# First stage of a six-stage decoder kernel: query weights in four column groups, and the loads and vector work in another order

## What is computed

```python
x = _layernorm(x + _L0_attn_ref(x, Wq, Wk, Wv, Wo))
x = _layernorm(x + _L0_xattn_ref(x, ctx, ...))
x = _layernorm(x + _L0_ffn_ref(x, ...))
x = _layernorm(x + _L1_attn_ref(x, ...))
x = _layernorm(x + _L1_xattn_ref(x, ctx, ctx, ...))
x = _layernorm(x + _L1_ffn_ref(x, ...))
```

```python
q = (x @ Wq).reshape(b, n, H, HD).transpose(0, 2, 1, 3)
k = (x @ Wk).reshape(b, m, HKV, HD).transpose(0, 2, 1, 3)
v = (x @ Wv).reshape(b, m, HKV, HD).transpose(0, 2, 1, 3)
q = q * cq + rotate_half(q) * cq
k = k * ck + rotate_half(k) * ck
attn = jax.nn.softmax(jnp.einsum('bhnd,bhmd->bhnm', q, k) * scale)
out = jnp.einsum('bhnm,bhmd->bhnd', attn, v)
return out.transpose(0, 2, 1, 3).reshape(b, n, H * HD) @ Wo
```

## Time and profile before

| | |
|---|---|
| time, median of 3 runs | 2896.91 us (2895.69 to 2898.89) |
| profiled execution, its own time | 2890.31 us |
| its span | 2888.5 us |
| PE busy | 2667.9 us, 92% |
| DVE, ACT, POOL busy | 1879.2, 1311.8, 1248.2 us |
| mean granted clock of PE | 0.965 |
| moved by DMA | 49.16 MB |

### The profile page before, as it was taken

How to read it: one execution, slowest core, us unless ns; L and a number is a source line. 1 busy time by engine, 2 the same in 40 slices (tenths; PEclk the granted TensorE clock), 3 DMA queues, 4 the chain that set the end, 5 groups by cost and what they waited for, 6 DMA issues and landing times. The chain is left out here.

```text
span 2888.5 us, 65059 instructions
## 1 busy us (share of the span) xinstructions
PE 2667.9 (92%) x23764; PEld 2306.1 (80%) x23764; DVE 1879.2 (65%) x4014; ACT 1311.8 (45%) x3138; POOL 1248.2 (43%) x1605
## 2 busy tenths in 40 slices
PE   6999999994999999999999889996999999699995
PEld 5999999994888888888888768885777777477774
DVE  5555556554777777777777654444777777366766
ACT  2222222223666666666666533332433334266665
POOL 3111121122576777777676501113455454334444
PEclk9999999997999999999999989997999999799998
DMA  4000000002000000000000020001000000000001
GB/s 144 8 7 7 4 7 7 7 0 99 6 4 5 4 4 5 4 5 4 5 4 5 0 75 0 0 0 33 9 8 11 7 11 0 26 27 26 29 12 59
DMA packets 42507, 49.16 MB, mean 17 GB/s; under 512 B 4032, under 2 KB 33600, under 8 KB 41920
## 3 DMA queue, kind: packets, MB, share of 16 engines
q1 hardware_dynamic: 42432, 48.16, 5.0%
HBM read 35.56 MB, written 4.19 MB: 14 GB/s over the span
## 5 line engine op out<-in xcount | busy, mean ns | idle before, releaser
L528 POOL TENSOR_TENSOR a_probs<-a_probs,a_rs 128x512 f32<-128x512 f32 x64 | 66.8, 1044 | 482.4 <-DVE a_rs L421 482.4
L1109 POOL TENSOR_TENSOR b_rows<-b_rows,b_swapped 128x512 f32<-128x512 f32 x160 | 204.4, 1286 | 56.0 <-DVE b_swapped L895 55.9
L1050 ACT ACTIVATE b_probs<-bank,b_shift,b_q_scale 128x128 f32<-128x128 f32 x512 | 228.2, 461 | 0.7
L1156 POOL TENSOR_TENSOR b_probs<-b_probs,b_rs 128x512 f32<-128x512 f32 x128 | 133.2, 1040 | 137.0 <-DVE b_rs L947 133.8
L2593 ACT ACTIVATE d_probs<-d_probs 128x512 f32<-128x512 f32 x128 | 78.9, 630 | 242.7 <-DVE d_probs L2492 240.8
L485 ACT COPY a_pT<-bank 128x512 f32<-128x512 f32 x64 | 37.5, 586 | 326.3 <-PE bank L300 326.3
L46 PE MATMUL bank<-a_xT,a_wq 128*128 128x256 f32 x512 | 150.3, 293 | 26.4 <-DVE a_xT L388 26.4
L1119 POOL TENSOR_TENSOR b_rms<-b_rms,sh_minus_half 128x8 f32<-128x8 f32 (+1 forms) x128 | 169.6, 1325 | 10.7
L903 DVE TENSOR_REDUCE b_ss<-b_squares 128x4 f32<-128x512 f32 x192 | 125.2, 680 | 73.7 <-ACT b_squares L1025 73.7
L46 PE MATMUL bank<-b_wo,b_oT 128*128 128x256 f32 x512 | 150.8, 295 | 1.4 <-DVE b_oT L869 1.4
L426 DVE TENSOR_TENSOR a_oT<-bank,a_oT 128x512 fp32r<-128x512 f32 x128 | 82.5, 686 | 103.2 <-ACT a_oT L490 103.2
(11 more groups left out here) (350 smaller groups left out, 8923.8 us busy)
## 6 DMA issues: line engine op xcount, KB each, us to landing
a_xT_in<-in_xT SPq DMA_DIRECT2D x16, 256.0 KB, 2.7
sh_x<-in_x SPq DMA_DIRECT2D x1, 4096.0 KB, 24.9
b_ctx_in<-in_ctxT SPq DMA_DIRECT2D x32, 128.0 KB, 2.0
d_x_in<-sh_x SPq DMA_DIRECT2D x16, 256.0 KB, 2.3
e_x_in<-sh_x SPq DMA_DIRECT2D x16, 256.0 KB, 2.3
e_cT<-in_ctxT SPq DMA_DIRECT2D x32, 128.0 KB, 2.5
out<-sh_x SPq DMA_DIRECT2D x16, 256.0 KB, 2.1
a_qT<-in_L_attn_Wq SPq DMA_DIRECT2D x1, 2048.0 KB, 8.5
```

The costliest lines, as they stand in the source:

```text
L1050: op = act.activation(probs[:, g % 2, keys], bS[:, keys], ACT.Exp, bias=shift[:, g % 2, a:a + 1], scale=q_scale[:, g, a // 2, a % 2:a % 2 ...
L1109: pool.tensor_tensor(rows[:, unit, :], rows[:, unit, :], swapped[:, half, :], ALU.add).then_inc(added[unit], 1)
L1156: pool.tensor_tensor(pr, pr, rs[:, g % 2, :].unsqueeze(2).to_broadcast([128, R, 128]), ALU.mult).then_inc(probs_ready[g], 1)
```

## The change

The loads. Wq is loaded in four groups of 512 columns, in the order group 0, x turned, group 1, the tables, groups 2 and 3, Wk, Wv, Wo. Then SP waits for the first low part of x, issues x turned of turn 1 and, behind it, x in rows. The 24 semaphore increments are made by ACT and POOL, 12 each.

The weights. Each group of Wq is folded (two DVE instructions over both chunks of rows), rounded and split by itself, and so is Wk; Wk's fold also takes two instructions instead of four. Wo is rounded on ACT, after Wv, and only its low part is made on POOL.

The order. DVE does `low_x(0)` after the first fold, and mixes the rest of the folds and low parts with the takes of turn 0. In turn 0 PE waits before each group of q, before k and before v for that group's low part alone. The wait on Wo moves from ahead of turn 1 into turn 1, to the `weigh_values` of turn 0's rows.

```diff
-        pieces = to_split(wk, folded_k, 1) + to_split(wq, folded_q, C) + to_split(wv, full_v, 1) + to_split(wo, full_o, 1)
-        w_loaded = [nc.alloc_semaphore(f"a_w_loaded{n}") for n in range(4)]
+        K, V, O = G, G + 1, G + 2
+        columns = [slice(g * R * HD, (g + 1) * R * HD) for g in range(G)]
+        pieces = [(wq[:, 0, :, columns[g]], wq[:, 1, :, columns[g]], folded[g]) for g in range(G)]
+        pieces += to_split(wk, folded[K], 1) + to_split(wv, full_v, 1) + to_split(wo, full_o, 1)
+        w_loaded = [nc.alloc_semaphore(f"a_w_loaded{n}") for n in range(len(pieces))]
...
         def _(sp):
-            for s in looped:
-                sp.sem_inc(s, 1)
...
+            def load_turn(i, source):
+                sp.wait_ge(x_low, nth(i - 1, 1, 1))
+                sp.dma_start(xT_in[:, :, :], source).then_inc(xT_loaded, 16)
+
+            load_turn(1, t["xT"][1])
             sp.dma_start(sh.x[:, :, :], t["x"].rearrange("(n p) d -> p n d", p=128)).then_inc(x_loaded, 16)
...
+            def needs(i, n):
+
+                if type(i) is int and i == 0:
+                    pe.wait_ge(w_ready, n + 1)
+
             def q_proj(i, g):
+                needs(i, g)
...
             def k_proj(i):
+                needs(i, K)
...
             def v_proj(i, r):
 
+                needs(i, V)
...
             def weigh_values(i, g):
+                if type(i) is int and i == 0:
+                    pe.wait_ge(wo_step, 1)
...
-            pe.wait_ge(w_ready, len(pieces) - 1)
             pe.wait_ge(zeroed, 1)
             turn(0, None, None)
-            pe.wait_ge(wo_step, 2)
             turn(1, 0, None)
...
+            def fold(n):
+                dve.wait_ge(w_loaded[n], 16)
+                halves = raw[n].rearrange("p c (h a e) -> p c h a e", a=2, e=HD // 2)
+                out = folded[n].rearrange("p c (h a e) -> p c h a e", a=2, e=HD // 2)
+                dve.tensor_tensor(out[:, :, :, 0, :], halves[:, :, :, 0, :], halves[:, :, :, 1, :], ALU.subtract).then_inc(w_folded, 1)
+                dve.tensor_tensor(out[:, :, :, 1, :], halves[:, :, :, 1, :], halves[:, :, :, 0, :], ALU.add).then_inc(w_folded, 1)
...
-            turn(0, None, None)
+            fold(0)
+            low_x(0)
+            fold(1)
+            low_w(0)
+            fold(2)
+            low_w(1)
+            dve.wait_ge(tables_loaded, 32)
+            take_q(0, None, 0)
+            fold(3)
+            low_w(2)
+            take_q(0, None, 1)
+            fold(K)
+            low_w(3)
+            take_q(0, None, 2)
+            low_w(K)
+            take_q(0, None, 3)
+            low_w(V)
+            take_k(0, 0)
+            take_k(0, 1)
             turn(1, 0, None)
...
+            for s in looped[1::2]:
+                act.sem_inc(s, 1)
             high_x(0)
+            for n in range(len(pieces)):
+                high_w(n)
             turn(0, None, 1)
...
+            for s in looped[0::2]:
+                pool.sem_inc(s, 1)
             pool.memset(sh.minus_half[:, :], -0.5).then_inc(zeroed, 1)
             pool.wait_ge(zeroed, 1)
-            split_on_pool(pool, pieces[-1], w_loaded[3], wo_step)
+            high, low, full = pieces[O]
+            pool.wait_ge(w_high, O + 1)
+            pool.tensor_tensor(low, full, high.bitcast(F32), ALU.subtract).then_inc(wo_step, 1)
             pool.wait_ge(x_loaded, 16)
```

More of the change, by code:

```diff
@@ L185, in self_attention_block @@
         with nc.sbuf_tensor("a_stage", [128, 2, C * H * HD], F32) as stage:
-            folded_q = stage[:, 0].rearrange("p (c n) -> p c n", c=C)
+            folded_q = stage[:, 0].rearrange("p (g c n) -> p g c n", g=G, c=C)
             full_o = stage[:, 1].rearrange("p (h n) -> p h n", h=H)
         oT = sb("oT", [128, 2, H, T2], F32R)
-        raw_q = qT[:, :, :, :, :].rearrange("p g b r q -> p (g b r q)").rearrange("p (c n) -> p c n", c=C)
-        raw_k = kT[:, :, :].rearrange("p g n -> p (g n)").rearrange("p (c n) -> p c n", c=C)
-        folded_k = probs[:, :, :]
+        raw = [qT[:, g, :, :, :].rearrange("p b r q -> p (b r q)").rearrange("p (c n) -> p c n", c=C) for g in range(G)]
+        raw.append(kT[:, :, :].rearrange("p g n -> p (g n)").rearrange("p (c n) -> p c n", c=C))
+        folded = [folded_q[:, g] for g in range(G)] + [probs[:, :, :]]
         full_v = v[:, :, :]
@@ L235, in _, with load_columns @@
         def _(sp):
-            for s in looped:
-                sp.sem_inc(s, 1)
-            sp.dma_start(raw_k, t["L0_attn_Wk"].rearrange("(c p) n -> p c n", p=128)).then_inc(w_loaded[0], 16)
+            def load_columns(g):
+                sp.dma_start(raw[g], t["L0_attn_Wq"].rearrange("(c p) n -> p c n", p=128)[:, :, columns[g]]).then_inc(w_loaded[g], 16)
+            load_columns(0)
             sp.dma_start(xT_in[:, :, :], t["xT"][0]).then_inc(xT_loaded, 16)
-            sp.dma_start(raw_q, t["L0_attn_Wq"].rearrange("(c p) n -> p c n", p=128)).then_inc(w_loaded[1], 16)
+            load_columns(1)
             sp.dma_start(cos[:, :], t["cosT"]).then_inc(tables_loaded, 16)
             sp.dma_start(sh.ident[:, :], t["ident"]).then_inc(tables_loaded, 16)
-            sp.dma_start(full_v, t["L0_attn_Wv"].rearrange("(c p) n -> p c n", p=128)).then_inc(w_loaded[2], 16)
-            sp.dma_start(full_o, t["L0_attn_Wo"].rearrange("(h p) n -> p h n", p=128)).then_inc(w_loaded[3], 16)
+            load_columns(2)
+            load_columns(3)
+            sp.dma_start(raw[K], t["L0_attn_Wk"].rearrange("(c p) n -> p c n", p=128)).then_inc(w_loaded[K], 16)
+            sp.dma_start(full_v, t["L0_attn_Wv"].rearrange("(c p) n -> p c n", p=128)).then_inc(w_loaded[V], 16)
+            sp.dma_start(full_o, t["L0_attn_Wo"].rearrange("(h p) n -> p h n", p=128)).then_inc(w_loaded[O], 16)
+            def load_turn(i, source):
+                sp.wait_ge(x_low, nth(i - 1, 1, 1))
+                sp.dma_start(xT_in[:, :, :], source).then_inc(xT_loaded, 16)
+            load_turn(1, t["xT"][1])
             sp.dma_start(sh.x[:, :, :], t["x"].rearrange("(n p) d -> p n d", p=128)).then_inc(x_loaded, 16)
-            with sp.Fori(1, n_turns) as i:
-                sp.wait_ge(x_low, nth(i - 1, 1, 1))
-                sp.dma_start(xT_in[:, :, :], t["xT"][bass.ds(i, 1), :, :, :].rearrange("a p c n -> (a p) c n")).then_inc(xT_loaded, 16)
+            with sp.Fori(2, n_turns) as i:
+                load_turn(i, t["xT"][bass.ds(i, 1), :, :, :].rearrange("a p c n -> (a p) c n"))
         @block.tensor
         def _(pe):
+            def needs(i, n):
+                if type(i) is int and i == 0:
+                    pe.wait_ge(w_ready, n + 1)
             def q_proj(i, g):
+                needs(i, g)
                 for u in range(2):
@@ L372, in _, with low_w @@
         def _(dve):
[L374 to L383, removed]
+            def fold(n):
[4 more added lines that the diff above has]
+                dve.tensor_tensor(out[:, :, :, 1, :], halves[:, :, :, 1, :], halves[:, :, :, 0, :], ALU.add).then_inc(w_folded, 1)
+            def low_w(n):
+                split_low(dve, pieces[n], n, w_high, w_ready)
             cos_b = cos[:, :].unsqueeze(1).to_broadcast([128, NB, S])
@@ L460, in _, with high_w @@
         def _(act):
-            for n, piece in enumerate(pieces[:-1]):
-                if n <= C:
-                    act.wait_ge(w_folded, 2 * C + 2 * n)
-                else:
-                    act.wait_ge(w_loaded[2], 16)
-                split_high(act, piece, w_high)
+            def high_w(n):
+                if n < V:
+                    act.wait_ge(w_folded, 2 * n + 2)
+                else:
+                    act.wait_ge(w_loaded[n], 16)
+                split_high(act, pieces[n], w_high)
             def high_x(i):
```

## The result

| | before | changed |
|---|---|---|
| median of 20 runs each | 2895.35 us | 2888.26 us |
| lowest to highest | 2889.12 to 2901.44 | 2882.78 to 2893.27 |
| the profiled execution's own time | 2890.31 | 2883.36 |
| its span | 2888.5 | 2881.6 |

The ratio is 0.9975, with an interval of 0.9968 to 0.9982: 7.2 us faster, between 5.2 and 9.3. I had forecast 14.3.

What follows compares the result with a forecast made beforehand. TensorE, busy 92% of the span, bounds the kernel, so only its idle time pays. PE starting at 9.1 instead of 25.56, less new waits, ends turn 0 14.3 us earlier: 2896.9 - 14.3 = 2882.6 us, range 2877 to 2890.

Steps and rivals of the forecast that it cites:

- The issue at 0.73: SP's first load, freed of the 24 increments, issues at 0.73 instead of 2.16 us: 1.43 us earlier for all loads.
- The first landing at 4.4: Wq's column group 0 lands 3.7 us after its issue at 0.73, as Wk did, so DVE can fold from 4.4.
- The durations: Turn 0: 512-element fold instructions 0.60 us each, Wo's rounding on ACT 3.65, PE waits of 1.1 and 0.9.
- rival C: DVE sets the pace: 512-element fold instructions cost 1.2 us, a pair 2.4; saving 10.7, time 2886.2 us; chance 8%.
- The clock: PE runs at 1.2 GHz for 5.5 us after its start (products 0.213 apart), then at 2.4 GHz through turn 0.
- Rival B: PE, served in pieces, stays at 1.2 GHz through turn 0; v ends at 39.7, saving 5.7, time 2891.2 us; chance 4%.
- signs of being wrong: Products 0.213 apart or clock below 1.00 after 16 us, fold pair 2.4, ACT's v copy or POOL's first multiplication waiting.
- Rival A: Loads pay their fixed time one after another; x in rows lands at 57.4, 7.1 us slower, 2904.0; chance 2%.
- What could be late next, cost 0: Wo's rounding on ACT, POOL's subtraction and multiplication, x in rows, PE's wait on Wo: all covered, 0 us.
- low V and a take end at 27.9, so v starts 0.15 late: End of turn 0: DVE delays v's products by only 0.15 us, and v's second unit ends at 31.0.
- its subtraction of 9.04 us: POOL's subtraction for Wo runs 26.0 to 35.0, leaving 1.0 us of cover before turn 1's first probability multiplication at 36.0.
- The sum: Turn 0's last product ends at 31.05 instead of 45.36, saving 14.3 us: 2896.9 becomes 2882.6 us.

Runs made afterwards that it cites:

- Wq by groups: Against four pieces with two folds a step earlier on DVE: each Wq column group in one stretch of memory; median 2880.09 us, ratio to before 0.9949.
- four pieces: Against the changed kernel: POOL forms Wo's low part in four pieces, each behind a multiplication of turn 1; median 2877.48 us, ratio to before 0.9934.
- early Wv: Against the changed kernel: DVE makes Wv's low part before the takes of q's last group; median 2880.27 us, ratio to before 0.9946.

## Why the prediction was right or wrong

**The issue at 0.73**: right, 0.74, and by itself worth 1.2 of the 1.43 us at PE's start and 1.45 at turn 1.

**The first landing at 4.4**: wrong by 1.2 us. I took Wk's 3.7 because bytes and row length agree. The group's rows lie 8 KB apart; with them together it is 3.9 (Wq by groups). That is most of PE's start at 10.39 instead of 9.1. Later loads were late too, under cover: Wo landed at 18.6 for 17.3, x in rows at 32.3 for 29.9.

**The durations**: right. Instructions of 512 elements start 0.60 apart, so rival C is out; Wo's rounding on ACT took 3.61 for 3.65, from 22.96 for 22.2; PE waited 1.07 and 0.56 for the forecast 1.1 and 0.9.

**The clock**: by the pace of the products, 0.213 us apart until then and 0.12 after, it rose at 14.6, after 4.2 us at the lower level, for the 5.5 I took, and held through both short waits. Rival B is out as I put it: the service in pieces did not hold the clock down. It fell once in turn 0, at 31.7, in a wait that I had not forecast. A granted clock below 1.00 after 16 us was one of my signs of being wrong, and it came, for another reason than B's.

**Rival A**: out. Eleven transfers behind the first did not pay in turn: x in rows, issued at 13.54, landed 18.8 us later, at 32.3 and not at 57, ahead of POOL's first multiplication (47.50). The 2.0 us that the prediction takes from the Trainium skill, page "DMA: Bandwidth & Descriptors", stand in its section "Anatomy of one DMA — SWDGE (gpsimd) path", on transfers issued by GpSimd; here SP issues them all.

**What could be late next, cost 0**: this is the step that failed, and with it the term before it, "low V and a take end at 27.9, so v starts 0.15 late": PE waited 8.51 us ahead of v, and v ended at 42.5 instead of 31.0. I had POOL's subtraction from 26.0 to 35.0 and DVE's low part of Wv in the same stretch, in neighbouring paragraphs, and went only by who waits for whom by semaphore. I counted "its subtraction of 9.04 us" as covered because nothing that it feeds was late. What it did cost is 8.6 us on DVE, and 2.1 more through the clock, and with both gone (four pieces) turn 1 starts 13.5 us earlier, of the 14.3. The kernel before could not warn by the subtraction's row: there DVE only took banks beside it, with one operand in PSUM. POOL's rounding could have: I took its 10.08 us for its own work, when 3.6 are.

The experiments show the mechanism: a DVE instruction with two SBUF operands and a POOL instruction that reads SBUF do not run beside each other; the one that starts second does its work when the first has ended. Three DVE rows (9.86, 2.65, 4.59 us) end 1.08, 0.55 and 1.07 us after POOL's end, and the POOL row (10.08 us) ends 3.46 after DVE's. Each time that is the instruction's own work (1.22, 0.69, 1.22 and 3.60 us) less 0.14 or 0.15. The Trainium skill states it, on the page "SBUF — State Buffer", section "Who interferes with whom": VectorE with two SBUF inputs reads the second through a port it shares with GpSimd, the lock is held for the whole instruction, and issue order decides who waits. The trace agrees that either engine can be the one held up, with the 9.86 us here and the 10.08 us of POOL's rounding before. It does not agree that issue order alone decides: the rounding is recorded from 18.68, ahead of DVE's instructions that start at 19.07, 23.48 and 24.61, and it still ended behind them all. I had not weighed that page.

**The sum**: 14.3 was nearly the right account of a kernel that does not have this conflict (13.5 at turn 1 with the four pieces, where turn 0's products started 1.3 us late and then took 21.5 us for the 21.9 I had). For the changed kernel's first stage it was about five times too large: 2.8 to 3.2 at turn 1. The measured 7.2 is more than that, and the rest I can't claim. It is also what brought the time into my range: 2895.35 less 2.8 is 2892.5, beyond the range's end at 2890. That the range held is luck.

## What to carry to other kernels

When work is moved in time, compare each stretch also for what the engines share, not only for semaphores: list POOL's long instructions that read SBUF, and see which DVE instructions with two SBUF operands now fall beside them. If they would meet, cut POOL's into pieces and put them where DVE reads PSUM: 8.9 us in four pieces of 2.4 left the length of turn 1 as it was here (35.28 us for 35.26). And a wait ahead of matmuls can cost more than itself: after the waits of 8.51 and 3.24 us the products of v ran at the lower clock and took 2.2 and 2.6 us more than before; after the wait of 2.79 us ahead of turn 1, with the early Wv, the granted clock was still 1.00.

## What the runs showed that I had not expected

A duration in the profile can hold a wait for another engine. POOL's rounding of 4096 elements was recorded with 10.08 us and takes 3.60; DVE's low part of Wv was recorded with 9.86 and takes 1.22. A row that ends about its own usual time after another engine's row does is the sign.

A load of 2 KB rows that lie 8 KB apart landed 4.9 us after its issue, one of as many rows in one stretch 3.8 and 3.9 (before: 3.7).

PE's clock rose 4.2 us after its first product in the changed kernel and 5.5 before, and fell 2.7 us into a wait of 8.51.

One kernel's executions differ by 15 us of 2900 (2885.51 to 2900.83 in 29 of the kernel before), and the mean granted clock goes with it. A gain of a few microseconds at the start is smaller than that, and the rows of the first stage tell it better than a few medians.
